# A one-core attention and mixture-of-experts kernel: a shorter grouping on VectorE, its counts' product ahead of a peel, and two peels of batch 1 moved behind the inversion

## The chip, the core and the metric

The kernel runs as one program on one core of a Trainium2 chip. A core has five engines with in-order queues of their own: TensorE (PE, matmuls; its weight loads are listed as PEld), VectorE (DVE), ScalarE (ACT), GpSimd (POOL) and SyncE (SP, which only issues DMAs here). Engines wait for each other through semaphores. The metric is the device time of one execution in microseconds (us).

## The reference

The input x is 8 batches of 512 tokens, 128 features each. Everything works on its normalised form xn.

```python
xn = _layernorm(x, axis=-1)
q = hidden_states @ Wq + bq                       # also k, v; 8 heads of 16
attn = softmax(q k^T / 4)                         # per head, 512 x 512
attn_out = (attn @ v1) - lam * (attn @ v2)        # then a layer norm, * 0.2, @ Wo + bo
...
h = jnp.mod(x_flat[:, :TOP_K].sum(axis=1).astype(jnp.int32), E)   # E = 8, TOP_K = 2
sel = jnp.stack([h, jnp.mod(h + 1, E)], axis=1)
y = jnp.maximum(x_flat @ W1e + b1e, 0.0) @ W2e + b2e              # for the two experts of a token
x = x + s * silu(y)
```

A token's expert h is the sum of its first two normalised features, cut toward zero to an integer, modulo 8. The second expert is the next one. So the 4096 tokens can be sorted by h, and each tile of 128 sorted tokens needs two neighbouring experts.

## The kernel before

One list of steps, `schedule()`, gives each step a time in units of one score tile. It is sorted once, and every engine walks the sorted list and emits its own part of each step. The numbers at the top of the file (`NORM_AT`, `PEEL_AT`, `TANH` and so on) are those times; they set only the order inside each engine's queue.

**Start-up.** DVE takes mean and variance of each batch (`stats`). POOL turns the variance into `rstd` with a power of -0.5 and the mean into `shift` (`shift`, groups of batches in `LN_GROUPS`). Batches 0 to 3 are normalised on ACT, batches 4 to 7 on POOL (`norm`), and SP stores each normalised batch to `xn_rows` in HBM (`store_xn`).

**Queries and keys.** For the scores, q and k are split in three bf16 parts (high, middle, low), stacked as 96 rows. For batches 0 and 1 the lower parts are *peeled*: PE repeats the f32 product (two passes), subtracts the parts it already has with a product against minus the identity, and ACT writes the rest as the next bf16 part (`project`, then `peel b i 1` for the middle and `peel b i 2` for the low part; i is 0 for q, 1 for k). SP spreads the parts with `stack_part`: one DMA for each of the twelve row blocks. A score of batch 0 needs all twelve.

**Grouping (routing).** `count_groups()` on DVE computes h for all tokens (32 columns of 128), a one-hot of 8 x 32, its counts (`count`) and a running count (`seen`). Step `route 1` is a small product on PE with `count`; `make_slots()` then gives every token its slot in sorted order. `find_tokens()` and `find_rows()` build two bf16 operands, and `invert` multiplies them on PE (32 small products) to turn slots into the list `inverse`. POOL then gathers sorted tiles from `xn_rows` by that list (`load_x`), but not before all eight `store_xn` have landed.

**The long part.** 256 scores, each followed by a maximum on DVE (`neg_max`), 24 scores later the exponential on ACT, and the product with the values (`pv_bank`) for every four. In between, 39 expert tiles: gather to `xs`, transpose (`turn_tile`), `hidden`, `down`; the first seven are extra tiles for the borders between groups, their results `z` go through `init_rows` in HBM, from which POOL fetches the starting value of `y_sb` for each of the 32 static tiles. ACT then takes the tanh, POOL the gate, and POOL scatters the tile to `y_rows`. Eight PSUM banks: two for scores, two for exponentials, one for `pv_bank`, three in a ring (`ring`) that all other products share in step order; a product waits until the reader of the bank's previous use is done.

`STACKS_BEHIND` makes SP's `stack_part` steps of batch 1 wait for the first `z` tile. SP and POOL issue in order: whatever waits in them holds all behind it.

## Time and profile before

| | us |
|---|---|
| time, median of 3 runs (lowest, highest) | 412.27 (411.48, 412.47) |
| the profiled execution, its own time | 411.52 |
| its span in the trace | 409.6 |
| PE busy, share of the span | 381.5, 93% |
| DVE busy | 291.8, 71% |
| ACT busy | 267.5, 65% |
| POOL busy | 189.3, 46% |

The profile counts an engine as busy from an instruction's start to its end; issuing DMAs and waiting are not busy. The span runs from the first to the last instruction that the trace shows. PE's clock is given as a share of its full 2.4 GHz: 1.00 or 0.50 (1.2 GHz). A chain of waits is followed back from the last instruction to what released it at each step. ACTq and SPq are the DMA issues of ACT and SP.

### The profile page before, as it was taken

The page shows a single profiled execution, that of the slowest core. Times are in us where ns is not written, and L with a number is a line of the kernel's source. Part 1 is how long each engine was busy: PE and PEld are TensorE (multiplying, and loading weights), DVE is VectorE, ACT ScalarE, POOL GpSimd, SP SyncE. Part 2 cuts the span into 40 slices and gives each one's busy share as a digit, 9 for nine tenths or more (in the row PEclk, how much of TensorE's full clock was granted, in tenths as well). Part 3 has the DMA queues.
Part 4 walks back from the last instruction along what each step waited for, and adds up shares of the span by engine and source line. Part 5 has one row for each costly group of instructions (what it writes and reads, how often), then busy time and mean ns, then how long its engine had stood idle before and what let it go on. Part 6 is the DMA issues. An engine that isn't in the chain of part 4 may idle for free.

```text
span 409.6 us, 8427 instructions
## 1 busy us (share of the span) xinstructions
PE 381.5 (93%) x2576; PEld 248.3 (61%) x2576; DVE 291.8 (71%) x758; ACT 267.5 (65%) x667; POOL 189.3 (46%) x262
## 2 busy tenths in 40 slices
PE   4996989999999999999999999999999999999993
PEld 2353876565775667766665668765676667764321
DVE  7787996656686757766676767866686767866884
ACT  3581756666765776576666767676766668675783
POOL 7944203454456543565355532663573444541200
PEclk9996999999999999999999999999999999999999
DMA  7975953263216451265105640346136141216740
GB/s 263 343 230 112 242 196 91 80 206 105 79 37 191 111 195 21 79 190 168 46 27 170 189 140 18 136 121 197 48 127 216 22 169 47 81 26 213 230 159 26
DMA packets 36945, 54.75 MB, mean 134 GB/s; under 512 B 6724, under 2 KB 25141, under 8 KB 36903
## 3 DMA queue, kind: packets, MB, share of 16 engines
q1 hardware_dynamic: 31456, 46.94, 34.6%
q0 software_dynamic: 3296, 6.76, 7.8%
q10 hardware_dynamic: 2151, 0.53, 0.6%
q8 instruction: 22, 0.36, 0.4%
q14 instruction: 20, 0.16, 0.1%
HBM read 15.59 MB, written 6.75 MB: 55 GB/s over the span
## 4 chain that ended last, share of the span: by engine, by line
PE 74%; DVE 7%; DMA 5%; ACT 4%; SPq 4%; issue 4%; POOL 1%; ACTq 0%; DVEq 0%; POOLq 0%
PE ring L1393 14%; PE pv_bank L1327 13%; PE ring L1414 12%; PE score L1289 12%; PE exp L1314 10%; PE ring L1251 3%; DVE neg_max L1049 3%; DMA xs<-xn_rows,inverse 3%; SPq L532 2%; PE ring L1335 2%; PE ring L1255 1%; PE ring L1353 1%; PE ring L1276 1%; PE ring L1375 1%; PE score L1264 1%
## 5 line engine op out<-in xcount | busy, mean ns | idle before, releaser
L1049 DVE TENSOR_REDUCE neg_max<-score 128x1 f32<-128x512 f32 x256 | 169.0, 683 | 72.3 <-PE score L1289 66.7
L1289 PE MATMUL score<-ks,qs 96*128 96x512 bf16 x256 | 98.3, 386 | 6.3 <-DVE neg_max L1049 6.0
L787 ACT ACTIVATE probs<-exp 128x512 f32<-128x512 f32 x124 | 72.5, 605 | 36.3 <-PE exp L1314 32.3
L787 ACT ACTIVATE xin<-exp 128x512 f32<-128x512 f32 x120 | 69.7, 604 | 38.5 <-PE exp L1314 38.1
L1314 PE MATMUL exp<-qs,ks 99*128 99x512 bf16 x244 | 91.7, 380 | 0.1
L825 ACT ACTIVATE hT<-ring,pair 128x128 f32<-128x128 f32 x256 | 73.4, 377 | 13.0 <-PE ring L1393 11.9
L1414 PEld LDWEIGHTS ring<-w_sb,hT 128*128 128x128 f32 x568 | 73.5, 191 | 10.4 <-issue 3.5
L1414 PE MATMUL ring<-w_sb,hT 128*128 (+1 forms) x568 | 75.4, 275 | 0.9 <-ACT hT L825 0.9
L1393 PEld LDWEIGHTS ring<-xsT,pair 128*128 128x128 f32 x512 | 66.3, 191 | 14.6 <-issue 8.1
L1393 PE MATMUL ring<-xsT,pair 128*128 128x128 f32 x512 | 68.2, 276 | 1.7 <-issue 1.2
L684 POOL TENSOR_SCALAR tanh<-tanh 128x128 f32<-128x128 f32 x32 | 17.2, 536 | 95.5 <-ACT tanh L845 95.2
L1289 PEld LDWEIGHTS score<-ks,qs 96*128 96x128 bf16 x256 | 25.9, 102 | 45.3 <-DVE neg_max L1049 24.0
L650 POOL DMA_INDIRECT xs<-xn_rows,inverse x39 | 38.5, 988 | 24.3 <-issue 10.2
L678 POOL DMA_INDIRECT y_sb<-init_rows,init_row x32 | 31.2, 974 | 29.0 <-DMA init_rows<-oT 17.3
L691 POOL DMA_INDIRECT y_rows<-y_sb,inverse x32 | 34.4, 1076 | 9.0 <-POOL y_sb L685 9.0
L1327 PE MATMUL pv_bank<-xin,va 128*32 128x512 f32 x256 | 31.2, 599 | 0.8 <-ACT xin L787 0.7
L1314 PEld LDWEIGHTS exp<-qs,ks 99*128 99x128 bf16 x244 | 23.9, 98 | 12.5 <-issue 1.9
L1327 PE MATMUL pv_bank<-probs,va 128*32 128x512 f32 x256 | 31.2, 599 | 0.0
L1174 DVE SCALAR_TENSOR_TENSOR y_sb<-ring,first_expert,y_sb 128x128 f32<-128x128 f32 x32 | 11.1, 348 | 15.2 <-PE ring L1375 8.7
L1251 PE MATMUL ring<-xT,wqk 128*128 128x512 f32 x32 | 18.0, 657 | 1.3 <-ACT xT L750 1.3
L845 ACT ACTIVATE tanh<-y_sb 128x128 f32<-128x128 f32 x32 | 9.8, 305 | 11.2 <-DVE y_sb L1176 11.1
L769 ACT ACTIVATE parts<-ring,qk_bias 128x512 bf16<-128x512 f32 x14 | 9.6, 689 | 9.7 <-PE ring L1251 9.7
(198 smaller groups left out, 417.4 us busy)
## 6 DMA issues: line engine op xcount, KB each, us to landing
pair<-table SPq DMA_DIRECT2D x32, 580.0 KB
qs<-parts SPq DMA_DIRECT2D x42, 128.0 KB
ks<-parts SPq DMA_DIRECT2D x42, 128.0 KB
xin<-_attn_hidden_states_dram SPq DMA_DIRECT2D x8, 256.0 KB, 4.4
table<-in_L_ffn_W_dram SPq DMA_DIRECT2D x2, 1024.0 KB, 9.2
w_sb<-in_L_ffn_W_dram SPq DMA_DIRECT2D x8, 256.0 KB, 10.4
xn_rows<-xn SPq DMA_DIRECT2D x8, 256.0 KB, 3.0
table<-_attn_hidden_states_dram SPq DMA_DIRECT2D x8, 256.0 KB, 5.4
```

Source lines behind the costliest of these rows:

```text
L650: pool.indirect_dma_start(xs[:, f % XS, :], None, xn_rows, bass.IndirectOffsetOnAxis(ap=inverse[:, f:f + 1], axis=0)).then_inc(tile_loaded ...
L678: pool.indirect_dma_start(y_sb[:, tile % YB, :], None, init_rows, bass.IndirectOffsetOnAxis(ap=init_row[:, tile:tile + 1], axis=0)).then_i ...
L691: pool.indirect_dma_start(y_rows, bass.IndirectOffsetOnAxis(ap=inverse[:, f:f + 1], axis=0), y_sb[:, tile % YB, :], None).then_inc(y_store ...
L787: a.activation(prob(n), exp_banks[n][:, :], ACT.Exp, scale=SCALE).then_inc(exp_done, 1)
L825: last = a.activation(hT[:, f % 2, FC * j + c, :], shared[:, c * P:(c + 1) * P], ACT.Relu, bias=bias)
L1049: v.tensor_reduce(neg_max[:, b % 2, col:col + 1], score_bank[n % 2][:, :], AX.X, ALU.max, negate=True).then_inc(max_taken, 1)
L1251: t.matmul(shared[:, :], wqk[:, i, :], xT[:, b % 2, :], start=True, stop=True).then_inc(shared_filled, 1)
L1289: t.matmul(score_bank[n % 2][:, :], qs[0:MAX_ROW, b % STK, hh, c * P:(c + 1) * P], ks[0:MAX_ROW, b % STK, hh, :], start=True, stop=True).t ...
L1314: t.matmul(exp_banks[n][:, :], ks[0:KROWS, b % STK, hh, kc * P:(kc + 1) * P], qs[0:KROWS, b % STK, hh, :], start=True, stop=True).then_inc ...
L1327: last = t.matmul(pv_bank[VW * i:VW * (i + 1), :], va[:, b % 2, kc, i, :], prob(4 * n4 + i), start=(kc == 0), stop=(kc == C - 1))
L1393: last = t.matmul(shared[:, c * P:(c + 1) * P], w1_chunk, xsT[:, f % 2, :], start=True, stop=True)
L1414: last = t.matmul(shared[:, half * D:(half + 1) * D], hT[:, f % 2, k, :], w2_chunk, start=(k % FC == 0), stop=(k % FC == FC - 1))
```

## The change

**The grouping.** The value v of a token is now formed from the means before `rstd` is there: DVE adds `-2 * mean` to the sum of the two features while POOL still works, so that a single multiplication is left behind `rstd`. Three casts between int32 and f32 go, since the operations beside them now read or write int32. The one-hot and the running count are laid one element apart, so that the running count comes out without the token itself and the subtraction after it goes. Half of `find_tokens` (`token[:, 1]`) moves from DVE to ACT, where it stands behind `project 1 1`. POOL computes `rstd` for batches 6 and 7 apart, and `shift` for batches 4 to 7 once, right ahead of their normalisation.

**The order.** The counts' product (`route 1`) goes ahead of `peel 0 1 2`; `norm 2` on ACT ahead of the first projections; on SP the stores of batches 2 and 4 to 7 go ahead of the last `stack_part` of batch 0; `peel 1 0 2` goes between scores 1 and 2, `peel 1 1 2` behind score 5, so that `invert` follows the middle peels. The three small DMAs that write ones into `ks` move from ACT's queue to SP's. `TX` lets the transposes of the extra tiles come earlier, `TANH` puts the tanh of a static tile later; that moves it behind one more exponential on ACT in 10 of 32 tiles. `INIT_AHEAD` and `SPLIT_MAX` shift two other steps in the list, and outside the start-up no engine's own instructions change order by them.

```diff
-LN_GROUPS = ((0, 1), (1, 2), (2, 4), (4, 6), (6, 8))
+LN_GROUPS = ((0, 1), (1, 2), (2, 4), (4, 6), (6, 7), (7, 8))
-NORM_AT = (-58, -56.4, -49.9, -47.93, -49.2, -49.1, -49, -48.95)
+NORM_AT = (-58, -56.4, -56.3, -47.93, -49.2, -49.1, -49, -48.95)
-PEEL_AT = (((-55.5, -55.3), (-55.4, -55.25)), ((-45.5, -45.3), (-45.4, -45.2)))
+PEEL_AT = (((-55.5, -55.3), (-55.4, -48.65)), ((-45.5, 1.5), (-45.4, 5.1)))
-TX, DX = 2.4, 3.2
+TX, DX = 3, 3.2
-TANH, GATE = 0.7, 1.84
+TANH, GATE = 1, 1.84
...
@@ SyncE and ScalarE: step "ones" moves from ACT to SP; new on ACT:
+                elif kind == "tokens":
+                    act.wait_ge(in_tile_ready, 1)
+                    a.activation(token[:, 1, :, :, :], in_tile, ACT.Copy, scale=row_of[:, 0:1]).then_inc(token_ready, 1)
@@ GpSimd, normalisation of batches 4 to 7
-                    pool.wait_ge(shift_ready, 1 + [b >= end for _, end in LN_GROUPS].index(False))
+                    if b == POOL_NORM[0]:
+                        tok = slice(C * b, NT)
+                        pool.wait_ge(rstd_ready, len(LN_GROUPS))
+                        link(g.tensor_scalar(shift[:, tok], mv[:, tok, 0], -1.0, None, ALU.mult))
+                        link(g.tensor_tensor(shift[:, tok], shift[:, tok], rstd[:, tok], ALU.mult))
@@ VectorE, count_groups
+                dve.wait_ge(rstd_ready, len(LN_GROUPS))
                 link(v.tensor_tensor(v01[:, :], v01[:, :], rstd[:, :], ALU.mult))
-                dve.wait_ge(shift_ready, len(LN_GROUPS))
-                link(v.scalar_tensor_tensor(v01[:, :], shift[:, :], 2.0, v01[:, :], ALU.mult, ALU.add))
...
-                link(v.tensor_copy(n_abs[:, :], whole_i))
-                link(v.tensor_tensor(over, n_abs[:, :], v_abs[:, :], ALU.is_gt))
-                link(v.tensor_tensor(n_abs[:, :], n_abs[:, :], over, ALU.subtract))
-                link(v.scalar_tensor_tensor(h[:, :], sign[:, :], -1.0, n_abs[:, :], ALU.add, ALU.mult))
-                link(v.tensor_copy(whole_i, h[:, :]))
-                link(v.tensor_scalar(whole_i, whole_i, EXP - 1, None, ALU.bitwise_and))
-                link(v.tensor_copy(h[:, :], whole_i))
+                link(v.tensor_tensor(over, whole_i, v_abs[:, :], ALU.is_gt))
+                link(v.tensor_tensor(n_abs[:, :], whole_i, over, ALU.subtract))
+                link(v.scalar_tensor_tensor(h_i[:, :], sign[:, :], -1.0, n_abs[:, :], ALU.add, ALU.mult))
+                link(v.tensor_scalar(h_i[:, :], h_i[:, :], EXP - 1, None, ALU.bitwise_and))
...
-                link(v.tensor_tensor_scan(flat, work[:, 512:768], zeros,
-                                          0.0, ALU.add, ALU.add))
-                v.tensor_tensor(seen[:, :, :], seen[:, :, :], onehot[:, :, :], ALU.subtract).then_inc(seen_ready, 1)
+                v.tensor_tensor_scan(work[:, 768:1024], work[:, 511:767], zeros,
+                                     0.0, ALU.add, ALU.add).then_inc(seen_ready, 1)
@@ TensorE, invert
-                    pe.wait_ge(token_ready, 1)
+                    pe.wait_ge(token_ready, 2)
```

PE's queue around the counts' product, before and then after; `ring<-count` is the counts' product, `ring<-xT,wqk` and `ring<-parts,minus_bf` are the f32 and the bf16 products of a peel, `ring<-ident,xn` is the transposition of batch 1.

```order
L1255 MATMUL ring<-xT,wqk 128x512
L1258 MATMUL ring<-parts,minus_bf 128x512 x2
L1255 MATMUL ring<-xT,wqk 128x512
L1258 MATMUL ring<-parts,minus_bf 128x512 x2
L1236 MATMUL ring<-ident,xn 128x128 x4
L1359 MATMUL ring<-count,before 128x8
L1360 MATMUL ring<-count,ones 128x8
L1251 MATMUL ring<-xT,wqk 128x512 x2
L1255 MATMUL ring<-xT,wqk 128x512
```

```order
L1257 MATMUL ring<-xT,wqk 128x512
L1260 MATMUL ring<-parts,minus_bf 128x512 x2
L1361 MATMUL ring<-count,before 128x8
L1362 MATMUL ring<-count,ones 128x8
L1257 MATMUL ring<-xT,wqk 128x512
L1260 MATMUL ring<-parts,minus_bf 128x512 x2
L1238 MATMUL ring<-ident,xn 128x128 x4
L1253 MATMUL ring<-xT,wqk 128x512 x2
L1257 MATMUL ring<-xT,wqk 128x512
```

The counts' product stood behind the low peel of k and the four transposes; now it stands ahead of both.

PE's queue around the inversion (`ring<-probs,qs`), before and then after; `score<-ks,qs` is a score, `ring<-ident,xs` the transposition of a gathered tile, `ring<-xsT,table` the first product of `hidden`.

```order
L1258 MATMUL ring<-probs,minus_bf 128x512
L1255 MATMUL ring<-xT,wqk 128x512
L1258 MATMUL ring<-probs,minus_bf 128x512 x2
L1255 MATMUL ring<-xT,wqk 128x512
L1258 MATMUL ring<-probs,minus_bf 128x512 x2
L1367 MATMUL ring<-probs,qs 128x78 x32
L1289 MATMUL score<-ks,qs 128x512 x6
L1375 MATMUL ring<-ident,xs 128x128
L1289 MATMUL score<-ks,qs 128x512 x2
L1375 MATMUL ring<-ident,xs 128x128
L1393 MATMUL ring<-xsT,table 128x128 x4
```

```order
L1260 MATMUL ring<-probs,minus_bf 128x512
L1369 MATMUL ring<-probs,qs 128x78 x32
L1291 MATMUL score<-ks,qs 128x512 x2
L1257 MATMUL ring<-xT,wqk 128x512
L1260 MATMUL ring<-probs,minus_bf 128x512 x2
L1291 MATMUL score<-ks,qs 128x512 x3
L1377 MATMUL ring<-ident,xs 128x128
L1291 MATMUL score<-ks,qs 128x512
L1257 MATMUL ring<-xT,wqk 128x512
L1260 MATMUL ring<-probs,minus_bf 128x512 x2
L1291 MATMUL score<-ks,qs 128x512
L1377 MATMUL ring<-ident,xs 128x128
```

The two low peels of batch 1 stood ahead of the inversion. One is now between scores 1 and 2; the other is behind the transposition of the first gathered tile and score 5.

SP's queue from the first stores to the weights, before and then after; `xn_rows<-xn` is `store_xn`, `qs<-parts` and `ks<-parts` are `stack_part` of batch 0, `w_sb<-in_L_ffn_W_dram` the loads of the remaining second weights.

```order
L541 DMA xn_rows<-xn 128x512 x2
L532 DMA qs<-parts 16x8x512 x3
L532 DMA ks<-parts 16x8x512 x3
L532 DMA qs<-parts 16x8x512 x2
L532 DMA ks<-parts 16x8x512 x2
L532 DMA qs<-parts 16x8x512
L532 DMA ks<-parts 16x8x512
L541 DMA xn_rows<-xn 128x512 x6
L502 DMA w_sb<-in_L_ffn_W_dram 128x4x128 x6
```

```order
L547 DMA xn_rows<-xn 128x512 x3
L533 DMA qs<-parts 16x8x512 x3
L533 DMA ks<-parts 16x8x512 x3
L533 DMA qs<-parts 16x8x512 x2
L533 DMA ks<-parts 16x8x512 x2
L533 DMA qs<-parts 16x8x512
L547 DMA xn_rows<-xn 128x512 x4
L533 DMA ks<-parts 16x8x512
L547 DMA xn_rows<-xn 128x512
L538 DMA ks<-ones_bf 3x8x512 x3
L503 DMA w_sb<-in_L_ffn_W_dram 128x4x128 x6
```

The last block of k stood ahead of six stores; now four of them (batches 4 to 7) stand ahead of it, and the store of batch 3 and the ones behind it.

## Rows read from the trace of the kernel before

**Rows 1.** The chain of waits, first 90 us: start, duration, engine, output, line.

```profile
31.45 4.89 DMA xs<-xn_rows,inverse
...
43.78 0.36 DVE oT L1167
...
44.62 0.62 SPq L532
...
65.26 3.53 DMA y_sb<-init_rows,init_row
...
69.57 0.69 DVE neg_max L1049
```

**Rows 2.** Windows: length, then busy us of PE, PEld, DVE, ACT, POOL; PE clock, DMA share, GB/s.

```profile
34.00:36.39 2.39, 0.00 (x1) 0.01 (x2) 2.02 (x10) 0.00 (x0) 0.95 (x1) 0.50 0.49 137
36.39:40.60 4.21, 4.21 (x16) 3.12 (x17) 1.79 (x3) 1.48 (x6) 1.89 (x2) 0.50 0.77 145
150.00:370.00 220.00, 216.61 (x1546) 148.07 (x1548) 153.13 (x368) 150.62 (x384) 111.17 (x139) 1.00 0.35 108
```

**Rows 3.** Timeline, grouping on POOL and DVE: start, duration, engine, line, operation, idle before.

```profile
8.14 1.04 POOL L631 TENSOR_TENSOR rstd<-var_eps,neg_half 128x4 f32<-128x4 f32 x1
...
15.21 1.67 POOL L631 TENSOR_TENSOR rstd<-var_eps,neg_half 128x8 f32<-128x8 f32 x1
...
16.91 0.17 DVE L1019 SCALAR_TENSOR_TENSOR shift<-mv,rstd 128x8 f32<-128x8 f32 x1 [2.00 <-POOL rstd L631]
...
17.98 0.28 DVE L897 CAST n_abs<-hT 128x32 f32<-128x32 int32 x1
...
19.42 0.18 DVE L903 CAST h<-hT 128x32 f32<-128x32 int32 x1
...
20.09 0.42 DVE L906 TENSOR_REDUCE count<-hT 128x8 f32<-128x256 f32 x1
...
20.43 0.75 DVE L909 TENSOR_TENSOR_SCAN hT<-hT 128x256 f32<-128x256 f32 x1
...
21.66 0.17 DVE L916 TENSOR_TENSOR_SCAN group_end<-ring,hT 128x8 f32<-128x8 f32 x1
...
26.79 0.54 DVE L948 TENSOR_SCALAR probs<-hT,row_of 128x1248 bf16<-128x1248 bf16 x1
```

**Rows 4.** Timeline, PE peels of batch 0 and ACT in the start-up.

```profile
18.09 1.02 PE L1255 MATMUL ring<-xT,wqk 128*128 128x512 f32 x2
...
19.38 1.02 PE L1255 MATMUL ring<-xT,wqk 128*128 128x512 f32 x2
...
21.46 0.59 ACT L750 ACTIVATE xT<-ring 128x512 f32<-128x512 f32 x1
...
24.05 1.64 ACT L755 ACTIVATE xn<-xin,shift,rstd 128x128 f32<-128x128 f32 x4
...
26.72 1.07 ACT L743 ACTIVATE table<-score 128x512 f32<-128x512 f32 x2
```

**Rows 5.** Timeline, ACT: its DMA issues, first copy of a gathered tile, a copy of 512.

```profile
34.46 2.46 ACTq L731 DMA_DIRECT2D ks<-ones_bf  x3
36.97 0.28 ACT L832 ACTIVATE xsT<-ring 128x128 f32<-128x128 f32 x1 [6.96 <-PE ring L1375]
...
48.34 0.65 ACT L735 ACTIVATE table<-table 128x512 f32<-128x512 f32 x1
```

**Rows 6.** Timeline of SP's issues, and the view of the tile `xn_rows`.

```profile
21.59 0.57 SPq L532 DMA_DIRECT2D ks<-parts  x1
23.60 3.07 SPq L541 DMA_DIRECT2D xn_rows<-xn  x6
...
DMA to landing us min/median/max: 2.1/3.0/8.1
```

**Rows 7.** Waits: engine, line, waited for, us in total, times, longest.

```profile
ACT tanh L845 <- DVE y_sb L1176: 11.1, 12, 1.8
...
PE ring L1375 <- DMA xs<-xn_rows,inverse: 3.0, 2, 2.4
```

More of the change, by code:

```diff
@@ L41 @@
 LAG = 24
[L43 removed]
+LN_GROUPS = ((0, 1), (1, 2), (2, 4), (4, 6), (6, 7), (7, 8))
 POOL_NORM = (4, 5, 6, 7)
 STATS_AT = (-60, -59, -58, -57, -56, -55, -54, -52)
[L46 to L47 removed]
+SHIFT_AT = (-58.5, -57.5, -55.5, -53.5, -53.4, -50)
+NORM_AT = (-58, -56.4, -56.3, -47.93, -49.2, -49.1, -49, -48.95)
 FOLD_QK_AT = -57.95
[L49 removed]
+QKV_AT = (-57.9, -48.62, 35, 67, 99, 131, 163, 181)
 PEELED = (0, 1)
 PROJECT_AT = ((-55.9, -55.6), (-47.95, -45.9))
[L52 to L53 removed]
+PEEL_AT = (((-55.5, -55.3), (-55.4, -48.65)), ((-45.5, 1.5), (-45.4, 5.1)))
+STACK_AT = (((-55.58, -55.45, -55.28), (-55.57, -55.35, -48.64)), ((12.1, 12.3, 12.5), (12.2, 12.4, 12.6)))
 BIAS_AT = -58.2
@@ L56 @@
 ROUTE_AT = (-48.8, -48.7)
-TOKENS_AT = -45
+TOKENS_AT = -45.6
 ROWS_AT = (-44, -43.9, -43.8)
@@ L60 @@
 INVERT_AT = -40
-EXTRAS_AT = 5.2
-GROUPS_AT = (9.05, 10.72, 13.05, 14.05)
+EXTRAS_AT = 4.7
+GROUPS_AT = (9.05, 10.72, 12.55, 14.05)
 STACKS_BEHIND = 1
@@ L72 @@
 FFN_PACE = 6.85
-TX, DX = 2.4, 3.2
+TX, DX = 3, 3.2
 PAIR_AT = (20, 21, 22)
-INIT_AHEAD = 1.5
+INIT_AHEAD = 1.67
 H1, D0, D1 = 1.8, 3.3, 4.5
 TT = 2
-SPLIT_MAX, TURN_MAX = 16.8, 18.9
+SPLIT_MAX, TURN_MAX = 16.5, 18.9
 EXP_OFF, PV_OFF = 0.05, 4
@@ L306, in gated_attention_moe @@
         sign = sb("sign", [P, NT])
-        h = sb("h", [P, NT])
+        h_i = sb("h_i", [P, NT], I32)
         count = sb("count", [P, EXP])
@@ L341, in gated_attention_moe @@
         inverse_f = cmp[:, 0:FT]
-        onehot = work[:, 512:768].rearrange("p (e t) -> p e t", e=EXP)
-        seen = work[:, 768:1024].rearrange("p (e t) -> p e t", e=EXP)
+        onehot = work[:, 511:767].rearrange("p (e t) -> p e t", e=EXP)
+        seen = work[:, 767:1023].rearrange("p (e t) -> p e t", e=EXP)
         zeros = work[:, 1024:1024 + EXP * NT]
@@ L429, in gated_attention_moe @@
         token_ready = sem("token_ready")
+        in_tile_ready = sem("in_tile_ready")
         slots_split = sem("slots_split")
@@ L533, in _ @@
                                          parts_of(b)[:, i, k, :]).then_inc(stacked[b % STK], 16)
+                elif kind == "ones":
+                    sp.wait_ge(dve_consts, 1)
+                    for slot_b in range(STK):
+                        sp.dma_start(ks[MAX_ROW:KROWS, slot_b, :, :],
+                                     ones_bf[:, :].unsqueeze(1).to_broadcast([PARTS, HEADS, S])).then_inc(ones_stacked, 16)
                 elif kind == "load_w2":
@@ L627, in _ @@
                     pool.wait_ge(stats_ready, end)
-                    if end < B:
+                    if first not in POOL_NORM:
                         g.tensor_scalar(shift[:, tok], mv[:, tok, 0], -1.0, None, ALU.mult)
@@ L632, in _ @@
                                     ALU.pow).then_inc(rstd_ready, 1)
-                    if end < B:
+                    if first not in POOL_NORM:
                         pool.wait_ge(rstd_ready, s[1] + 1)
@@ L727, in _ @@
                     act.dma_start(lnb_sb[:, :], ln_b.rearrange("(p a) -> p a", a=1)).then_inc(small_loaded, 16)
-                elif kind == "ones":
-                    act.wait_ge(dve_consts, 1)
-                    for slot_b in range(STK):
-                        act.dma_start(ks[MAX_ROW:KROWS, slot_b, :, :],
-                                     ones_bf[:, :].unsqueeze(1).to_broadcast([PARTS, HEADS, S])).then_inc(ones_stacked, 16)
                 elif kind == "copy_ninth":
@@ L860, in _ @@
             v.memset(zeros, 0.0)
+            v.memset(work[:, 767:768], 0.0)
             link(v.memset(va[:, :, :, :, HD:VW], 0.0))
@@ L945, in find_tokens @@
                 dve.wait_ge(slots_split, 1)
-                link(v.tensor_tensor(in_tile, by_pair(slot_tile[:, 0:NT], FT), over_pairs(columns[:, :, :], NT // 2), ALU.is_equal))
-                v.tensor_tensor(token[:, 0, :, :, :], in_tile, by_pair(ordinal[:, :], FT), ALU.mult)
-                v.tensor_scalar(token[:, 1, :, :, :], in_tile, row_of[:, 0:1], None, ALU.mult).then_inc(token_ready, 1)
+                v.tensor_tensor(in_tile, by_pair(slot_tile[:, 0:NT], FT), over_pairs(columns[:, :, :], NT // 2),
+                                ALU.is_equal).then_inc(in_tile_ready, 1)
+                dve.wait_ge(in_tile_ready, 1)
+                v.tensor_tensor(token[:, 0, :, :, :], in_tile, by_pair(ordinal[:, :], FT), ALU.mult).then_inc(token_ready, 1)
             def find_rows(q):
@@ L1014, in _ @@
                         continue
-                    tok = slice(C * first, C * end)
-                    v.tensor_tensor(v01[:, :], xin[:, :, 0], xin[:, :, 1], ALU.add).then_inc(pair_summed, 1)
-                    dve.wait_ge(rstd_ready, g + 1)
+                    link(v.tensor_tensor(v01[:, :], xin[:, :, 0], xin[:, :, 1], ALU.add))
                     dve.wait_ge(stats_ready, end)
-                    v.scalar_tensor_tensor(shift[:, tok], mv[:, tok, 0], -1.0, rstd[:, tok],
-                                           ALU.mult, ALU.mult).then_inc(shift_ready, 1)
+                    v.scalar_tensor_tensor(v01[:, :], mv[:, :, 0], -2.0, v01[:, :],
+                                           ALU.mult, ALU.add).then_inc(pair_summed, 1)
                 elif kind == "transpose_x" and s[1] not in PEELED:
```

6 lines of the change are left out of this document (1 added, 5 removed).

## The prediction

> **What bounds the kernel now.** I read four views, in this order. The page's busy shares (in the table) give PE 93% of the span, DVE 71%. The windows say where: from 150 to 370 us PE is busy 216.61 of 220 us [rows 2], so that stretch is PE's own work, and the change leaves all of it in place. What is left is the start. There the chain of waits [rows 1] runs from the inverse list through the first gather (31.45 us, 4.89 us to land), the first z result (43.78), SP's queue of `stack_part` issues behind it (from 44.62), and the gather of the first `y_sb` (65.26, 3.53 long) to a maximum at 69.57, on which the next score waits. From there on PE hardly waits. Last the timeline: between 34 and 36.39 us PE does nothing, since the first gather has not landed, and from 34.00 to 40.60 its clock is 0.50 [rows 2]. So the change can save what it takes off the time of the first gather, and what it spares of the slow clock; it pays with what it puts behind the gather.
>
> **The grouping on POOL and DVE.** A power over 8 columns takes 1.67 us on POOL, one over 4 takes 1.04 [rows 3]. Batches 6 and 7 apart cost 2.08 instead of 1.67, and one more addition and its wait (about 0.3), but the `shift` pair of batches 4 and 5 (about 0.55 with its waits) goes from this place. I put `rstd` at 17.1 instead of 16.9: +0.2. Behind it DVE has one multiplication where it had three operations in two steps: about -0.3. The three casts go. The first is 0.28, the one at 19.42 is 0.18 [rows 3], the third I take like that; with 0.03 to 0.04 for each link that is 0.75. So the counts, ready at 20.51 (20.09 + 0.42), are ready at 19.67. The running count starts 0.34 behind the start of the counts and takes 0.75 [rows 3]: it ends at 20.34. The subtraction is gone. The slots' first operation, at 21.66 [rows 3], needs the running count's engine and the counts' product.
>
> **The counts' product ahead of a peel.** Two low peels of batch 0 start at 18.09 and 19.38, 1.29 apart [rows 4]; PE is through with the first at about 19.4, so it waits for the counts until 19.67, and its product of two small pairs takes some 0.6: 20.3. DVE's slots start at 20.4 instead of 21.66, -1.26. The half of the token operands at 26.79 (0.45 from start to start of the next) leaves DVE. Its row operands, which ended at about 29.65, end at 27.95: DVE alone would bring the inversion forward by 1.7.
>
> What it costs on PE: the peel behind it starts at 20.4 instead of 19.38, +1.0, and with it the transposes of batch 1, their copy on ACT (21.46 in rows 4, now about 22.45) and the first projection of batch 1, now done at 24.1.
>
> **ACT decides the inversion.** Behind that projection ACT writes its high part (to 24.8), normalises batch 3 (1.64 [rows 4], to 26.3), writes the second high part (to 26.9), and only then has the token operands. Their 1248 elements are in no row: ACT's copy of 512 from SBUF takes 0.65 and one of 128 takes 0.28 [rows 5], 0.95 ns an element, so 1.3 us; the bounds are 1.1 and 1.6 (0.65 times 1248/512). Nearest to the slope of the two rows, I take 1.3: ready at 28.15. PE has been idle since about 27.3; DVE's rows have been there since 27.95. The 32 products take 1.3 with nothing between them, so the inversion is over at 29.55 instead of 30.60. From there to POOL's gather it was 0.85. The gather starts at 30.4: **-1.0**.
>
> The other gate of the gather is the stores. On SP the stores of batches 4 to 7 wait for POOL, whose last normalisation now ends at 26.05 (one `shift` pair, 0.9 later than now). Then come the last block of k (0.57), and the store of batch 3 at 27.25. A store lands 2.1 us (least) or 3.0 (median) after its issue [rows 6]: 29.35 to 30.25. Just under the inversion; at 8.1, the longest, this gate would decide, but that one fell in the initial loads. Score 0 needs that block of k too (29 to 29.7), and the bias copies on ACT (1.07 and two small ones [rows 4], now from 28.7 to 29.9): it starts at 29.9 instead of 30.4. The ones' 2.46 us of issue [rows 5] leave ACT; there they ended at 36.9, with the first copy of a gathered tile at 36.97. But ACT's other ten issues start 1.3 later, at 30.6, and end at 35.75, with the low part of `peel 1 0 2` behind them (to 36.4). The first copy is at 36.4: -0.6, which hides, because PE has a peel to do.
>
> **The two peels.** `peel 1 0 2` costs 1.29 us of PE at 30.4 and lies wholly in the wait for the gather. `peel 1 1 2` does not: it stands behind the first tile's transposition, now at 35.4, and ahead of the first `hidden`. It puts **+1.3** on PE there, at full clock. Two quantities then say when the long part starts:
> - PE's backlog: -1.0 (gather), +1.3 (peel), and, if the clock holds, minus what the slow clock cost: 4.21 us of work at 0.50 between 36.39 and 40.60 [rows 2] is 2.1 us lost. Sum -1.8.
> - The chain over z and SP: the first `hidden` would end at 38.6 instead of 39.6, and the first z come at 42.8 instead of 43.78; SP's queue and the `y_sb` gather follow by the same -1.0, as nothing in SP's order changes there.
>
> The later of the two decides at 69.57, and PE's lead counts where the chain has slack: between -1.0 and -1.8 I take **-1.3**. The earlier transposes of the extra tiles (`TX`) I price at nothing; they take no time off PE, and between -0.4 and +0.2 from the waits ahead of `hidden`. `TANH` moves 10 tanh behind an exponential. ACT waited 12 times for `y_sb`, 11.1 us in all [rows 7], and some of that goes, but the exponentials behind them delay PE nowhere that the rows show: 0, with -0.4 and a loss (below) as bounds.
>
> The profiled execution took 411.52, its span 409.6. 411.52 - 1.3 = 410.2; the median of the runs lies 0.75 above that execution, so **411.0** (-0.3%). Its own range is 410.2 to 411.9.
>
> **Does the clock hold?** It is 0.50 from 34.00 on, where PE does nothing for 2.4 us [rows 2]; it came back when PE had worked for 4.2 us. In the changed kernel a peel lies in that stretch, and the gap before the gather lands is 2.2 us instead of 2.4. The Trainium skill (TensorE: Matmul & The Clock Gate, "HAM oscillation — how this bites in real kernels") warns of this very pattern, a matrix engine that waits for a transfer between pieces of work and finds itself throttled. [...]
>
> **Rivals.**
> - *The clock falls again (20%).* The gap is nearly as long, and the engine does the peel of k at 1.2 GHz: 2.6 us instead of 1.3. PE works at half rate from 35.4 to about 40.6, 5.2 us instead of 4.2: -1.0 + 1.3 + 0.5 = +0.8. Time 413.1, with 412.6 to 413.8. For it: the gap. Against it: the peel in front of it.
> - *The whole gain of DVE comes through (13%).* If ACT reaches the token operands earlier than I think, the inversion is bound by DVE's rows: -1.7 at the gather, and as the clock holds -2.2 at the end: 410.0. Against it: ACT's normalisation of batch 3 stands in front.
> - *The gain is swallowed (10%).* From 44 us SP issues without a pause, and DVE has one maximum more behind the gather; if the stores land late (3.0 us and more behind 27.25) or the z chain waits on DVE, the long part starts when it did: 412.1.
> - *The late tanh makes gathers late (12%), the case on the slower side.* POOL's queue holds gate, scatter and then the gather of the tile after next. A tanh behind one more exponential is up to 0.6 us later, and that gather with it. PE waited for a gather twice, 3.0 us in all, 2.4 of it the first gather [rows 7]; so once after it, 0.6: the margins are there but not large. Past 0.13 us a tile in 10 tiles the 1.3 is gone; at 0.3 us a tile it is +3.0 - 1.3 = +1.7: 414.0.
>
> **From the cases to the numbers.** My forecast has 45%. A difference of 0.3% is 1.24 us, about what a measurement of this kernel can tell from no change. Faster by more: 25 of the 45, and the 13 of the full gain, 38%. Slower by more: 8 of the 20 of the clock and the 12 of the tanh, 20%. Within: 42%. Eight in ten lie between 409.8 (most of the full gain) and 413.8 (the clock's upper end; beyond it most of the tanh case).
>
> **What would show it.** In the new profile: counts' product at 19.7 to 20.3 on PE; DVE's slots at 20.4; ACT's token operands at 26.8, 1.3 long, and PE waiting for them; the first gather at 30.4, released by DVE's `inverse` and not by a store; a clock of 1.00 between 34 and 41; the first z at 42.8 and the first `y_sb` at 67.9; the same number of PE waits for gathers after 110 us. The forecast is wrong if the gather starts within 0.3 us of 31.45, if the clock row shows 0.50 for longer than 6 us, or if PE's waits for `xs` after 70 us grow past 1.5 us.

## The result, and the profile after

The changed kernel takes 414.80 us (median of 8 runs, 414.01 to 417.62), the kernel before 412.37 beside it (8 runs, 411.48 to 412.68). The ratio is 1.0082 [1.0064, 1.0100]: **slower by 0.8%**, above the range of 409.8 to 413.8. Its profiled execution took 414.82, its span 413.0 against 409.6. The ratios of this document leave out executions in a slower state (one of ten in `e1_dve_waits`, at 769.6 us, and one of eight in `e2_k_first`, at 446.8).

The long part is as it was. From 150 to 370 us PE is busy 216.21 us, where it was 216.61 [rows 2]. Of the 3.4 us by which the span grew 3.0 lie ahead of it, and the chain of waits shows them (start, duration, engine, output, line):

```profile
15.88 1.05 POOL rstd L637
...
17.70 11.14 POOL xn L650 x16
28.86 0.32 SPq L547
...
29.22 0.56 SPq L533
...
29.83 0.60 SPq L547
...
47.62 0.62 SPq L533
...
68.30 3.54 DMA y_sb<-init_rows,init_row
...
72.60 0.69 DVE neg_max L1051
```

SP's stack starts 3.0 us later than in [rows 1] (47.62 for 44.62), and so do the first `y_sb` gather (68.30 for 65.26) and the maximum behind it (72.60 for 69.57). So 3.0 of the 3.4 us are there by 47 us. They begin at the chain's head, with POOL's sixteen normalisations, which take 11.1 us. POOL's timeline, of before and then of after (start, duration, engine, line, operation, count, idle before):

```profile
16.87 8.19 POOL L640 TENSOR_SCALAR xn<-xin,rstd,shift 128x128 f32<-128x128 f32 x16
31.45 1.22 POOL L650 DMA_INDIRECT xs<-xn_rows,inverse  x1 [6.39 <-DVE inverse L1141]
```

```profile
17.70 11.13 POOL L650 TENSOR_SCALAR xn<-xin,rstd,shift 128x128 f32<-128x128 f32 x16
...
25.41 2.56 POOL L650 TENSOR_SCALAR xn<-xin,rstd,shift 128x128 f32<-128x128 f32 x1
...
35.30 1.22 POOL L660 DMA_INDIRECT xs<-xn_rows,inverse  x1 [6.47 <-issue]
```

They start 0.8 later, but end 3.8 later (28.83 for 25.06). One of the sixteen takes 2.56 us where the median is 0.46; the one ahead of it takes 0.99 and the last one 0.87. Together that is 3.0 us more than three medians. DVE's timeline shows what ran beside it, before and after:

```profile
25.22 0.81 DVE L946 TENSOR_TENSOR hT<-hT,columns 128x1248 bf16<-128x1248 bf16 x1
26.06 0.81 DVE L947 TENSOR_TENSOR probs<-hT,ordinal 128x1248 bf16<-128x1248 bf16 x1
```

```profile
24.16 0.94 DVE L949 TENSOR_TENSOR hT<-hT,columns 128x1248 bf16<-128x1248 bf16 x1
25.13 0.94 DVE L952 TENSOR_TENSOR probs<-hT,ordinal 128x1248 bf16<-128x1248 bf16 x1
26.00 2.51 DVE L957 TENSOR_TENSOR qs<-hT,grid 128x1536 bf16<-128x1536 bf16 x3
```

In the kernel before, POOL was done at 25.06 and DVE's operands began at 25.22: they missed each other by 0.16 us. Now DVE's operands are 1.06 earlier, POOL's last normalisations are later, and they lie side by side. DVE's products take 0.94 instead of 0.81, POOL's normalisation waits. On a small scale the two had met before: in the kernel before, one normalisation took 0.73 us, from 22.44, beside DVE's f32 products of 128x256, and the longest of the sixteen took 0.81. One that fell into DVE's reduction, which reads a single tensor, took 0.44 (the view of the tile `xn`, least, median and longest in ns, and the two timelines, before):

```profile
L640 POOL TENSOR_SCALAR xn<-xin,rstd,shift x16: 443/457/807, 16.9 to 24.6; 128x128 f32<-128x128 f32 x16
```

```profile
23.48 0.60 DVE L925 TENSOR_REDUCE slot_f<-hT 128x32 f32<-128x256 f32 x1
```

```profile
23.75 0.44 POOL L640 TENSOR_SCALAR xn<-xin,rstd,shift 128x128 f32<-128x128 f32 x1
```

SP carries it on (timeline of SP, after):

```profile
22.46 6.72 SPq L547 DMA_DIRECT2D xn_rows<-xn  x4
29.22 0.56 SPq L533 DMA_DIRECT2D ks<-parts  x1
29.83 0.60 SPq L547 DMA_DIRECT2D xn_rows<-xn  x1
```

Behind the store of batch 7 stand the last block of k and the store of batch 3. That last store landed 4.2 us after its issue, where the kernel before had 3.1: at 34.06, and POOL issues the first gather at 35.30 instead of 31.45. Between that landing and the gather lie another 1.24 us; it is the same 1.24 in the other four profiles whose gather waits for a store (e2, e7, e11, e12), while behind DVE's `inverse` it is 0.30 (before). PE meanwhile (after):

```profile
28.41 1.48 PE L1369 MATMUL ring<-probs,qs 128*128 128x78 bf16 x32 [0.83 <-ACT probs L758]
33.23 1.03 PE L1291 MATMUL score<-ks,qs 96*128 96x512 bf16 x2 [3.35 <-DMA ks<-parts]
```

The inversion is over at 29.89, 0.7 earlier than before. Then PE waits 3.35 us for the block of k, and the clock falls in that wait, at 31.5, ahead of the peels; it is back at 38.4 (windows, after):

```profile
31.60:34.00 2.40, 0.77 (x2) 0.47 (x3) 0.13 (x1) 0.00 (x0) 0.00 (x0) 0.50 0.80 221
34.00:36.39 2.39, 2.39 (x5) 0.79 (x4) 1.16 (x2) 0.00 (x0) 1.09 (x1) 0.50 0.28 66
36.39:40.60 4.21, 3.85 (x13) 1.22 (x10) 3.11 (x10) 1.21 (x3) 2.97 (x4) 0.77 0.21 58
```

### The profile page after: what moved, and what is told of

Read it like the earlier page. It is cut to its first block, busy times and chain, and to the rows that moved or that the text cites. A ratio compares the mean times of both kernels' runs of the same rounds, so it can differ in the third digit from the quotient of the medians.

```text
span 413.0 us, 8425 instructions
## 1 busy us (share of the span) xinstructions
PE 382.3 (93%) x2576; PEld 247.7 (60%) x2576; DVE 291.0 (70%) x753; ACT 268.3 (65%) x668; POOL 193.9 (47%) x264
## 4 chain that ended last, share of the span: by engine, by line
PE 72%; POOL 7%; SPq 6%; issue 6%; DVE 4%; DMA 3%; ACT 2%; ACTq 0%; POOLq 0%; DVEq 0%
PE pv_bank L1329 14%; PE ring L1395 13%; PE ring L1416 12%; PE score L1291 12%; PE exp L1316 10%; POOL xn L650 3%; PE ring L1253 3%; DVE neg_max L1051 2%; POOL rstd L637 2%; SPq L533 2%; PE ring L1337 2%; PE ring L1355 2%; PE ring L1278 1%; DMA xs<-xn_rows,inverse 1%; SPq L503 1%
## 5 line engine op out<-in xcount | busy, mean ns | idle before, releaser
L695 POOL TENSOR_TENSOR y_sb<-tanh,y_sb 128x128 f32<-128x128 f32 x32 | 14.6, 457 | 2.7
L1329 PEld LDWEIGHTS pv_bank<-xin,va 128*32 128x32 f32 x256 | 6.5, 109 | 15.6 <-issue 10.3
```

The costliest lines, as they stand in the source:

```text
L1329: last = t.matmul(pv_bank[VW * i:VW * (i + 1), :], va[:, b % 2, kc, i, :], prob(4 * n4 + i), start=(kc == 0), stop=(kc == C - 1))
```

## The experiments

Theory A: POOL's normalisation and DVE's products with two tensor inputs keep each other from a port to SBUF, and so the stores come late. Its rivals blame SP's order, or DMA traffic. The twelve runs, each as a ratio to the kernel before on the same chip (e1 to e4 ran on one chip, e5 to e8 together, then e9 to e11, and e12):

| run | ratio to before [95%] | first gather issued |
|---|---|---|
| `e1_dve_waits` | 0.9989 [0.9964, 1.0013] | 31.02 |
| `e2_k_first` | 1.0073 [1.0053, 1.0093] | 34.26 |
| `e3_code_only` | 1.0046 [1.0022, 1.0069] | 32.27 |
| `e4_order_only` | 1.0050 [1.0025, 1.0074] | 31.42 |
| `e5_pool_beside` | 1.0000 [0.9982, 1.0018] | 31.51 |
| `e6_act_takes_7` | 1.0012 [0.9991, 1.0034] | 30.61 |
| `e7_after_again` | 1.0103 [1.0075, 1.0131] | 37.05 |
| `e8_wait_and_peel` | 1.0025 [1.0005, 1.0046] | 31.17 |
| `e9_wait_peel_first` | 0.9953 [0.9930, 0.9976] | 31.06 |
| `e10_act7_peel_first` | 0.9979 [0.9951, 1.0006] | 30.61 |
| `e11_gaps_in_rows` | 1.0039 [1.0008, 1.0069] | 36.09 |
| `e12_small_late` | 1.0075 [1.0048, 1.0102] | 33.15 |

### Apart in time, or another order on SP

`e1_dve_waits`, DVE starts its operands only behind POOL's last normalisation:

```diff
                 dve.wait_ge(slots_split, 1)
+                dve.wait_ge(xn_ready[B - 1], 1)
```

> The changed kernel with one wait added: VectorE starts the bf16 operands of the inversion only when GpSimd has normalised batch 7. Theory A (GpSimd's normalisation and VectorE's two-input bf16 operations keep each other out): the 16 normalisations take 8.3 us again instead of 11.1 and end at 26.0; VectorE's operands run from 26.1 to 30.0; the first gather is issued at 31 to 32 instead of 35.3; time 412 to 412.8, in spite of an operand start that is 1.9 us later. Theory B (only SP's order, the last k block behind the stores, costs): the normalisations still take 11 us, the later operands cost on top, time 415 to 416.5.

`e2_k_first`, the last block of k ahead of the stores of batches 4 to 7 on SP:

```diff
-STACK_AT = (((...), (-55.57, -55.35, -48.64)), ...
+STACK_AT = (((...), (-55.57, -55.35, -49.25)), ...
```

> The changed kernel with SP's last k block of batch 0 issued ahead of the stores of batches 4 to 7 again. Theory A: score 0 starts at about 30 instead of 33.2, but the normalisations still end at 28.8 and the gather is still issued at 34.5 to 35; time 413.5 to 414.5. Theory B: the scores' start is what was lost; time 411 to 412.

`e3_code_only` is the changed code with the old table of times, `e4_order_only` the old code with the new table (with the old grouping of the powers).

> The changed code with the old table of step times (only the half of the token operands that ACT makes stands where the changed table has it): the shorter grouping without the new order. The counts' product stays behind the peel and the transposes, so VectorE's operands start near 24.8 to 25.2. Theory A: part of the collision, since the normalisations start 0.8 us later and the operands a little earlier: they end at 26.5 to 27.5, gather at 31.5 to 32.5, time 412.3 to 413.3. Theory B: SP's order is the old one, so 411.5 to 412.3.

> The old code with the new table of step times (the groups of rstd left as they were): the new order without the shorter grouping. Theory A: normalisations start at 16.9, operands at about 24.7, little collision, they end at 25.1 to 25.8; gather at 30.5 to 31.5; time 411.5 to 413. Theory B: the last k block stands behind the stores as in the changed kernel; time 414 to 415.

The wait takes 1.7 us of DVE's time and makes the kernel 0.9% faster than the changed one, by the two ratios to before, which come from two chips. That is a little better than I expected. POOL and DVE in `e1_dve_waits`:

```profile
17.57 7.93 POOL L650 TENSOR_SCALAR xn<-xin,rstd,shift 128x128 f32<-128x128 f32 x16
31.02 1.22 POOL L660 DMA_INDIRECT xs<-xn_rows,inverse  x1 [5.52 <-DVE inverse L1144]
```

```profile
25.60 0.81 DVE L950 TENSOR_TENSOR hT<-hT,columns 128x1248 bf16<-128x1248 bf16 x1 [1.72 <-POOL xn L650]
```

The sixteen take 7.93, the products 0.81, and the gather is released by `inverse` and no longer by a store. With the block of k first, score 0 starts at 30 us as the prediction wanted, but the sixteen still take 11.00, the gather is still at 34.26, and the time stays up: SP's order alone is not the cause. A ratio of 1.0073 is 415.4 us beside 412.37, above the 414.5 of theory A, which I had expected.

The two halves are each 0.5% slower, and neither has the 2.56 us. In `e3_code_only` the operands begin at 25.06 and only the last normalisation meets them (0.99 us); ACT's token product, though, now stands ahead of the peel copies that PE waits for (0.66 and 0.46 us), PE's inversion ends at 31.4, and the gather comes 0.8 late. In `e4_order_only` the gather is on time, but the clock has fallen when PE comes to the moved peel (two rows of PE's timeline):

```profile
37.22 1.91 PE L1255 MATMUL ring<-xT,wqk 128*128 128x512 f32 x2
38.93 1.05 PE L1258 MATMUL ring<-probs,minus_bf 128*128 128x512 bf16 x2
```

At full clock the same rows are 1.02 and 0.59. The peel takes 2.6 us instead of 1.3, and SP's stack starts at 46.19. Both halves are slower than theory A had them. Beside 412.37 the ratio of `e4_order_only` is 414.4 us, the time that theory B had forecast, but not by its reason: the block of k is not late there, and score 0 starts at 30.39.

### The port by itself

`e5_pool_beside`, the kernel before with three more normalisations on POOL:

```diff
                     last.then_inc(xn_ready[b], 1)
+                    if b == POOL_NORM[-1]:
+                        for t in range(3):
+                            g.tensor_scalar(spare[:, t, :], xin[:, C * b + t, :], ..., ALU.mult, ALU.add)
```

> The kernel before, with three more normalisations of the same form on POOL (128x128 float32, into a spare tile that nobody reads) right behind the last real one, which ends at 25.06: they fall beside DVE's two-input bf16 products, which begin at 25.22. POOL has nothing else to do until 31.4, so no wait of the kernel changes. Theory A (a DVE product with two tensor inputs and a POOL normalisation keep each other from the memory port, whoever holds it finishes): at least one of the three takes over 1.5 us against 0.46, together they end after 27.5 instead of 26.45, and DVE's products lengthen by 0.1 to 0.2 each (0.81 to 0.94). Theory B (the 2.56 us of the changed kernel was something of that kernel alone: the new semaphore, ACT's product, DMA traffic): three times 0.46, ending at 26.45, DVE's 0.81 unchanged. Both: total within 0.3% of before, at most +0.3 us.

POOL's three, and DVE's operands (timelines, and the tile `spare` with least, median and longest in ns):

```profile
L646 POOL TENSOR_SCALAR spare<-xin,rstd,shift x3: 457/991/1288, 25.1 to 26.5; 128x128 f32<-128x128 f32 x3
```

```profile
25.28 0.94 DVE L951 TENSOR_TENSOR hT<-hT,columns 128x1248 bf16<-128x1248 bf16 x1
26.25 0.94 DVE L952 TENSOR_TENSOR probs<-hT,ordinal 128x1248 bf16<-128x1248 bf16 x1
27.12 0.54 DVE L953 TENSOR_SCALAR probs<-hT,row_of 128x1248 bf16<-128x1248 bf16 x1
27.58 2.51 DVE L958 TENSOR_TENSOR qs<-hT,grid 128x1536 bf16<-128x1536 bf16 x3
```

```profile
26.53 1.29 POOL L646 TENSOR_SCALAR spare<-xin,rstd,shift 128x128 f32<-128x128 f32 x1
```

The first begins at 25.11, 0.17 ahead of DVE's first product, and takes 0.46; the next two take 0.99 and 1.29. So the effect is there without any of the changed code, as theory A has it, though my bound of 1.5 us was too high. DVE's two products go from 0.81 to 0.94; the one with a single tensor input stays at 0.54. But it doesn't let POOL through: the second normalisation ends 0.32 us behind the first product, the third 0.62 behind the second product, at 27.82, which is 0.16 behind the end of the single-input one. The time is unchanged: what POOL does there, nobody waits for.

`e11_gaps_in_rows`, the changed kernel with a gap between the three row products:

```diff
                                 over_pairs(...), ALU.is_equal).then_inc(at_row_ready, 1)
+                dve.wait_ge(at_row_ready, q + 1)
```

> The changed kernel with DVE waiting for its own end between the three row products (a gap of some 0.1 us between them, as there is between its first two products, where they took 0.94 each and POOL's normalisation came through in 0.99). Theory A, as it stands now (POOL comes to the port only in a gap between DVE's products, and products issued without a gap shut it out for their whole length): no normalisation takes over 1.7 us (2.56 now), the three products take 0.85 to 0.95 each, the last normalisation ends by 28.3 instead of 28.8, the first gather is issued 0.5 or more earlier, ratio to before 1.003 to 1.008. Rival (gaps play no part; POOL loses the port for as long as DVE has work of this kind): the longest normalisation stays at 2.4 us or more, ratio 1.008 or above.

```profile
L650 POOL TENSOR_SCALAR xn<-xin,rstd,shift x16: 447/474/1778, 17.8 to 27.2; 128x128 f32<-128x128 f32 x16
```

The longest is 1.78 instead of 2.56 and ends at 27.23, 0.24 behind the first row product, in whose shadow it had stood: where DVE waits for a semaphore between two products, POOL comes in. The products behind one another without such a wait had kept it out for two and a half of them. The sixteen end at 28.36, 0.5 earlier. That is theory A's direction, with its bounds narrowly missed (1.7 for the longest, 28.3 for the end; the second row product took 1.01). The gather was not earlier in this profile (36.09, with a landing of 5.5 us, below), and the ratio of 1.0039 is lower than those of the changed kernel, 1.0082 and 1.0103 on other chips, with an interval that meets the first of theirs.

### The stores' landing

The other term of the delay: the last store's time from issue to landing. Where it was issued at 26.4 to 26.9 it was 2.1 to 2.8 us (e1, e6, e8, e9, e10); at 29.1 to 29.8 it was 3.9 (e2), 4.2 (after), 5.5 (e11) and 6.2 (`e7_after_again`, the changed kernel once more, beside e6 and e8, with 1.0103 a little above what I expected):

> The changed kernel itself, beside the others on one chip, for ratios on the same chip. Expected 1.007 to 1.009 of before.

Beside the late stores travel ACT's ten loads of constants, 27.6 to 33.0. `e12_small_late` takes them away:

```diff
-SMALL_AT = -45.1
+SMALL_AT = 4.6
```

> The changed kernel with ACT's ten loads of small constants (lambdas, value and output weights, biases; 27.6 to 33.0 in its profile) issued behind the second peel copy instead, after 36. The stores that the first gather waits for landed 4.2 and 6.2 us after their issue at 29.8 and 29.6 in two profiles of the changed kernel, against 2.1 to 2.8 where they were issued at 26.4 to 26.9. Theory A (being late, they travel together with these loads): the last store lands within 3.2 us and the first gather is issued at 34.3 or before (35.3 and 37.05 in the two profiles). Rival (their company is the k block and the rows of ones of SP's own queue, which stay): landing 3.8 or more, gather at 35 or later. The loads now delay ACT's copies of the turned tiles by up to 5 us behind the gather, so the total is no test: 1.004 to 1.015.

The store at 29.55, and the gather:

```profile
L547 SPq DMA_DIRECT2D xn_rows<-xn x1: 596/596/596, 29.6 to 29.6; - x1
...
  POOL xs L660: 4.6, 1
...
DMA to landing us min/median/max: 2.4/2.4/2.4
```

```profile
33.15 1.22 POOL L660 DMA_INDIRECT xs<-xn_rows,inverse  x1 [4.59 <-issue]
```

2.4 us, issued as late as in the changed kernel. The gather is at 33.15 instead of 35.30 and 37.05. The block of k points the same way: PE waits 1.82 us for it, where it waits 3.35 (after), 3.71 (e7) and 3.36 (e11). So being late seems to cost twice: 2.8 us of normalisation, and 1.8 to 3.8 us of landing beside loads of which only the first few had been issued when the stores landed in time. This second part rests on one profile against three, and a landing of 4.2 us alone proves nothing: in `e12_small_late` itself the three stores issued at 22.1 to 23.8, with none of these loads near, took 4.1 to 4.2, and in `e5_pool_beside` the last store, issued at 25.5, took 4.3. Only the 5.5 and the 6.2 lie outside what stores took without that company. As expected the total says nothing (ACT's first copy of a gathered tile waits for the loads until 39.88).

### Taking the work off, and the two peels

`e6_act_takes_7` (normalisation of batch 7 on ACT, in a gap of 1.2 us, `shift` released to ACT by a semaphore):

```diff
+ACT_TOO = 7
-NORM_AT = (..., -49, -48.95)
+NORM_AT = (..., -49, -48.3)
@@ GpSimd
-                elif kind == "norm" and s[1] in POOL_NORM:
+                elif kind == "norm" and s[1] in POOL_NORM and s[1] != ACT_TOO:
...
@@ ScalarE
-                elif kind == "norm" and s[1] not in POOL_NORM:
+                elif kind == "norm" and (s[1] not in POOL_NORM or s[1] == ACT_TOO):
...
```

> The changed kernel with the normalisation of batch 7 on ACT, between its copy of batch 1's transpose (ends 23.1) and its first projection (24.33, for which it sits idle 1.2 us now): POOL keeps twelve. Theory A: POOL's twelve take 0.46 each and end near 23.4, ahead of DVE's first product at 24.2, so none is stretched and DVE does not wait; ACT's 1.64 us delay its token product by 0.45 (27.03 to 27.5), inversion over at 30.3, first gather near 31.1 (changed kernel 35.3, before 31.45). Time 0.998 to 1.000 of before, 4 to 5 us under the changed kernel. Theory B (stores late by their order on SP or by their landing under other traffic): gather still at 33 or later, ratio 1.004 or more.

```profile
17.63 6.17 POOL L652 TENSOR_SCALAR xn<-xin,rstd,shift 128x128 f32<-128x128 f32 x12
30.61 1.22 POOL L662 DMA_INDIRECT xs<-xn_rows,inverse  x1 [6.80 <-DVE inverse L1145]
```

```profile
35.98 0.47 PE L1379 MATMUL ring<-ident,xs 128*128 128x128 f32 x1 [2.66 <-DMA xs<-xn_rows,inverse]
36.25 0.63 PE L1293 MATMUL score<-ks,qs 96*128 96x512 bf16 x1
36.68 1.91 PE L1259 MATMUL ring<-xT,wqk 128*128 128x512 f32 x2
```

POOL ends at 23.8 and DVE is not slowed. The gather is issued at 30.61, 0.84 ahead of [rows 1], and 0.2 from my forecast of 30.4. But its tile is there at 35.98, only 0.4 earlier than in [rows 2], and in this profile the clock had fallen, so the peel behind it, from 36.68 to 39.19, costs 2.5 us. Without the collision, what the change brings is about the price of its second peel: the ratio is 1.0012, within measurement of no change, where I had expected 0.998 to 1.000.

`e8_wait_and_peel`: as e1, with `peel 1 0 2` back ahead of the inversion. `e9_wait_peel_first`: as e1, with `peel 1 1 2` ahead of the turn of the first gathered tile. `e10_act7_peel_first`: the same in e6.

```diff
-PEEL_AT = (..., ((-45.5, 1.5), (-45.4, 5.1)))
+PEEL_AT = (..., ((-45.5, -45.3), (-45.4, 5.1)))       # e8
+PEEL_AT = (..., ((-45.5, 1.5), (-45.4, 4.4)))         # e9, e10
```

> The changed kernel with DVE's wait for POOL's last normalisation ahead of its operands, and besides with the third piece of batch 1's q block back ahead of the inversion (instead of between scores 1 and 2), where PE stood idle 1.09 us. With the wait alone the first gather was issued at 31.02. Theory A (PE's idle time before the inversion is there because DVE's rows end late): the 1.24 us of the piece fit, inversion at most 0.2 later, and scores 2 to 4 come 0.9 earlier behind it; but PE then has less to do between the scores and the first gather, so the clock falls as in the kernel before, which gives back some 2 us: ratio 1.000 to 1.004. Rival: the piece between the scores is worth nothing for the clock, and the time is that of the wait alone, 0.998 to 1.000.

> The changed kernel with DVE's wait for POOL's last normalisation, and the third piece of batch 1's k block moved ahead of the turn of the first gathered tile (it stood behind score 5). With the wait alone PE stood idle from 33.3 to 35.98 for the gather, and the piece then cost 1.24 us behind it at full clock and more where the clock had fallen. Theory A (PE's idle time there is pure waiting for the gather, and work in it is free): the piece runs 33.3 to 34.7, the copy of the first turned tile is not later, everything behind the gather comes 1.2 earlier, and PE's idle stretch shrinks to 1.3 us, so the granted clock stays at 1.00 in more of the executions: ratio 0.993 to 0.998 of before. Rival (the work behind the gather is bound by DVE and ACT or by the second gather, not by PE): ratio 0.998 to 1.001, like the wait alone.

> The same move of that piece in the kernel whose batch 7 is normalised on ACT (ratio 1.0012 without it, the clock at 0.50 from 36 to 39 in its profile and the piece taking 2.6 us there). Theory A: 0.994 to 0.999. Rival: 1.000 to 1.003.

PE in `e9_wait_peel_first`, then three windows of it:

```profile
33.62 1.02 PE L1258 MATMUL ring<-xT,wqk 128*128 128x512 f32 x2
34.48 0.59 PE L1261 MATMUL ring<-probs,minus_bf 128*128 128x512 bf16 x2
35.64 0.33 PE L1378 MATMUL ring<-ident,xs 128*128 128x128 f32 x1 [0.56 <-DMA xs<-xn_rows,inverse]
```

```profile
34.00:36.00 2.00, 1.44 (x6) 0.45 (x5) 1.79 (x9) 1.17 (x2) 0.77 (x1) 1.00 0.54 148
36.00:38.00 2.00, 1.69 (x11) 1.11 (x10) 1.84 (x4) 0.55 (x2) 1.15 (x2) 1.00 0.17 47
38.00:40.60 2.60, 2.60 (x23) 2.35 (x23) 2.20 (x4) 2.24 (x10) 1.40 (x2) 1.00 0.88 252
```

The peel now runs in PE's idle time, the tile finds PE free, and the clock is at 1.00 throughout. SP's stack starts at 43.08, 1.5 earlier than in [rows 1]. **0.9953: `e9_wait_peel_first` beats both kernels**, the changed one by 1.3 to 1.5% if the ratios of different chips are set side by side. Against `e1_dve_waits` (0.9989) the intervals overlap; what the peel's move saves is read from the timelines: the first product of `hidden` starts at 37.26 instead of 38.22, SP's stack at 43.08 instead of 44.04. That its place between the scores was right for the other peel shows in e8: ahead of the inversion it costs nothing there (gather 31.17, against 31.02), but the clock falls between 34 and 36 us (0.86, then 0.50 to 38), and the ratio goes from 0.9989 to 1.0025. These two intervals overlap, and they come from two chips, so of e8 I take only the clock row and the direction. e10 came out within its expectation too, but its interval touches 1, and it does not tell whether ACT or the wait is the better cure.

## Why the prediction was wrong

**The grouping on POOL and DVE** was right: last `rstd` at 16.92 (17.1 forecast), counts ready at 19.58 (19.67), slots at 20.55 (20.4). **The counts' product** ran from 20.00 to 20.5 (19.7 to 20.3 forecast).

**ACT and the inversion** were right. ACT's token product began at 27.03 and took 1.32 (1.3, from the slope of two rows), PE waited for it, and the inversion ended at 29.89 (29.55).

**The step that failed** is the one about the stores: "the stores of batches 4 to 7 wait for POOL, whose last normalisation now ends at 26.05 (one `shift` pair, 0.9 later than now)". I moved POOL's sixteen by a time and kept their length. They ended at 28.83, 2.8 us later. The term was mis-sized because it was taken by itself: I had worked out that DVE's operands come 1.3 to 1.7 earlier and that POOL's work ends 0.9 later, and never put the two on one axis, where they cross. What crosses there is a shared resource. DVE's product with two tensor inputs and POOL's normalisation don't run together: 0.46 becomes 0.87 to 2.56 on POOL, 0.81 becomes 0.94 on DVE, with the changed code (after, e11) or without it (e5), and not where they are apart (e1, e6). This is the rule of the Trainium skill (SBUF — State Buffer, "Who interferes with whom"): VectorE and GpSimd share one pair of ports, as an exclusive lock that the one that starts first holds for its whole instruction, and an instruction of VectorE with two inputs in SBUF contends with a GpSimd instruction that reads SBUF, one with a single input outside the two-port modes does not. The traces agree with both halves as far as they go: every two-input bf16 product beside POOL's work shows it, and a reduction with one input left POOL at 0.44. DVE's bf16 `tensor_scalar` has one input too, and yet in `e5_pool_beside` POOL came out only behind it; whether it ran in such a two-port mode no run here shows. What the traces add is the length: through products that follow each other without a semaphore between them POOL waited for more than one.

**The landing** was the second miss, in the same step. I bounded it by [rows 6], 2.1 to 3.0 us, and set the 8.1 aside as one of the initial loads. The bound held for the last store where it was issued at 26.1 to 27.6 (2.0 to 3.1). At 29.8 the same store took 4.2 us or 6.2; in e12, with ACT's loads out of the way, 2.4. And I let the gather follow the landing at once, while 1.24 us lie between them in every profile in which a store released it: by that, my own landing at 30.25 would have put the gather at 31.5, and not "Just under the inversion".

All of it together: last store issued 2.6 later than forecast (29.83 for 27.25), landed 1.2 to 3.2 longer than the median of [rows 6], 1.24 more to the gather, and the first gather at 35.30 where 30.4 was forecast.

**The two peels.** `peel 1 0 2` is hidden where the scores are on time (e1), and e8's clock row speaks for its place; in the changed kernel it ran at half clock (1.91 us from 34.05 where 1.02 is full clock). `peel 1 1 2` at +1.3 was right at full clock (in the changed kernel it ran from 38.86 to 40.15, the clock being back); e9's timeline shows that none of it need be paid.

**-2.1 for the clock spared** holds only where the stores are on time. In the changed kernel PE waited for the block of k, and the clock went down at 31.5 instead of 34.0 and stayed at 0.50 for 6.8 us. More than 6 us was one of my signs of a wrong forecast, but a poor one: in the kernel before it is 6.8 us as well, from 34.0 to 40.8. I had also taken the idle stretch for the reason of the old fall. But in the kernel before the clock fell at 34.0, where that stretch only begins; ahead of it, from 31.60 to 34.00, PE had worked 1.56 us of 2.40 in four short scores. With the wait (e1) the profile shows 1.00 from 33.3 to 40.6, and five of nine executions keep it (mean clock 0.998 or more, 408.4 to 409.3 us); the others, 0.992 to 0.996, take 409.9 to 411.7. The kernel before on that chip never exceeds 0.996. So this was neither -2.1 nor 0 but came and went from one execution to the next; the medians of the two kinds lie 1.6 us apart.

**The sum.** Even with the collision gone no run reaches the forecast of -0.3% with the peels where the change puts them: -0.1% in e1, whose interval still holds it, and +0.1% in e6, whose interval does not. Of the 0.84 at the gather in e6 0.4 arrives, since the transfer lands at nearly the same time, and the peel behind it takes that back.

**The rivals.** "The gain is swallowed" named the place, stores that land late, but priced it at the height of no change (412.1): it only let the gain go and did not follow the delay further than the old gather. "The clock falls again" happened as well, as a consequence. For the late tanh nothing speaks. PE's waits for gathered tiles behind 70 us did grow, from 0.6 us to 1.9, past the 1.5 that I had named as a sign, but they are 0.5 in `e1_dve_waits`, which has the late tanh, and 2.1 in `e3_code_only`, which has the old one. Of my signs the releaser of the first gather was the best: it was to be `inverse` and not a store, and that it is not is the first thing that the profile shows. The list of what would prove me wrong looked for a gather near 31.45 only, and not for one 3.9 us behind it.

## What to carry to other kernels

When a change makes one engine earlier and another later, lay both timelines on one axis and look for what comes to overlap that did not: VectorE products of two SBUF tensors beside GpSimd work is such a pair, and here 0.16 us had kept them apart. A transfer's landing time, read from a trace, was measured at one moment of issue; if the issue moves, allow a wider range (here 2.0 to 6.2 us for stores of one size) and ask what else is travelling then. And work that has to stand near a wait goes ahead of it, not behind: the same peel took 1.3 to 2.6 us of PE behind the gather's wait, and ahead of it it ran in idle time.

## What the hardware showed that I had not expected

- A POOL `tensor_scalar` of 128x128 float32, 0.46 us alone, took 0.99 where it began beside one DVE bf16 product of two tensors, 1.29 with a single-input bf16 `tensor_scalar` behind that product, 1.78 across two products issued without a wait between, and 2.56 across three. Why POOL was let in ahead of the third row product in the changed kernel, and behind the `tensor_scalar` in e5, with no semaphore there, no run tells.
- DVE pays too, but little and evenly: 0.13 us for each product of 0.81 while POOL has work.
- The same 256 KB store to HBM, issued at 29.1 to 29.8, landed in 2.4 us with SP's own transfers beside it (one profile) and in 3.9 to 6.2 with ten small loads from ACT's queue as well (four). Issued at 22.1 to 27.6, with at most the first few of these loads behind them, such stores took 2.0 to 4.3.
- The first gather was issued 1.24 us behind the landing of the last store where that store released it (five profiles), and 0.30 behind `inverse` where DVE did.
- The length of an idle stretch alone does not tell whether PE's clock falls: it stayed at 1.00 behind 2.73 us in e1's profile and fell at 35.7, 0.3 us ahead of the end of a stretch of 2.66, in e6's.
